# Attention of a macaron block: one division for two groups of heads, places from a running count

## What is computed

```python
q1, q2, k1, k2 = projections of x and of x with the token before   # 16 heads, 4 numbers each
L_q, L_k = exterior(q1, q2), exterior(k1, k2)                      # 6 numbers a head, normed
attn = jnp.einsum('bqhc,bkhc->bhqk', L_q, L_k @ J6.T) * 6 ** -0.5
attn = softmax(where(causal, attn, -inf))                          # over the keys
out = einsum('bhqk,bkhd->bqhd', attn, (x @ W_v + b_v) by heads)    # 16 numbers a head
x = x + out @ W_o + b_o
```

## Time and profile before

| | us |
|---|---|
| median of 3 runs | 1180.17 (1180.03 to 1180.23) |
| the profiled execution, its time | 1177.99 |
| the profiled execution, its span | 1176.3 |
| PE busy in the span | 1036.9 (88%) |
| ACT busy | 884.8 (75%) |
| DVE busy | 774.8 (66%) |
| POOL busy | 435.5 (37%) |
| mean granted clock of TensorE | 0.982 of full speed |

### The profile page before, as it was taken

How to read it: one execution, slowest core, us unless ns; L and a number is a source line. 1 busy time by engine, 2 the same in 40 slices (tenths; PEclk the granted TensorE clock), 3 DMA queues, 4 the chain that set the end, 5 groups by cost and what they waited for, 6 DMA issues and landing times.

```text
span 1176.3 us, 23514 instructions
## 1 busy us (share of the span) xinstructions
PE 1036.9 (88%) x7487; PEld 557.7 (47%) x7487; DVE 774.8 (66%) x1565; ACT 884.8 (75%) x1314; POOL 435.5 (37%) x531
## 2 busy tenths in 40 slices
PE   4998999898886888998889898988889998999996
PEld 3457999755553211222122122222123568898854
DVE  6897777768996314443244557476579778777866
ACT  4336777646888999999999999989998336677720
POOL 1004666377720323321111122430121435577755
PEclk9999999989998899999999999999999999999998
DMA  8902555446766101010201022020200854566655
GB/s 289 289 27 60 166 172 167 144 121 197 214 193 215 52 20 53 19 50 10 64 10 46 23 69 76 22 80 8 58 1 1 272 185 149 158 185 186 178 170 152
DMA packets 125716, 133.78 MB, mean 114 GB/s; under 512 B 13224, under 2 KB 111888, under 8 KB 125616
## 3 DMA queue, kind: packets, MB, share of 16 engines
q1 hardware_dynamic: 109056, 90.95, 24.5%
q0 software_dynamic: 14448, 39.47, 12.2%
q10 hardware_dynamic: 2112, 2.10, 0.5%
HBM read 80.43 MB, written 52.04 MB: 113 GB/s over the span
## 4 chain that ended last, share of the span: by engine, by line
PE 25%; ACT 23%; issue 19%; DVE 9%; POOL 2%; DVEq 1%; DMA 1%; ACTq 0%; POOLq 0%
ACT wide L2021 21%; PE banks L2388 6%; PE banks L2313 4%; PE banks L1905 3%; PE banks L2400 3%; PE banks L1880 2%; POOL f_region L1341 2%; PE banks L2322 2%; PE banks L1919 1%; PE banks L2376 1%; DVE x_res L1595 1%; DVE wide L1622 1%; DVEq L2596 1%; PE banks L1433 1%; DVE attn_lines_parts L202 1%
## 5 line engine op out<-in xcount | busy, mean ns | idle before, releaser
L2021 ACT ACTIVATE wide<-banks 128x1536 f32<-128x1536 f32 (+1 forms) x448 | 505.5, 1282 | 14.6 <-PE banks L1880 14.4
L1905 PE MATMUL banks<-wide,attn_attend_v_now 128*32 128x512 f32 (+3 forms) x2560 | 298.6, 542 | 0.1
L2037 POOL TENSOR_SCALAR_AFFINE_SELECT wide<-wide 128x512 f32<-128x512 f32 (+2 forms) x176 | 89.5, 523 | 444.3 <-ACT wide L2021 443.9
L1880 PE MATMUL banks<-attn_attend_q_now,attn_attend_k_now 32*128 32x512 f16 (+3 forms) x1280 | 158.8, 357 | 68.1 <-ACT wide L2021 64.3
L1880 PEld LDWEIGHTS banks<-attn_attend_q_now,attn_attend_k_now 32*128 32x128 f16 x1280 | 43.2, 91 | 321.2 <-ACT wide L2021 297.6
L651 POOL DMA_INDIRECT f_region<-xn_rows,f_token_of x79 | 79.1, 1001 | 126.0 <-DVE f_token_of L882 83.7
L2388 PE MATMUL banks<-f_xnt 128*128 128x128 f32 x752 | 101.7, 278 | 9.8 <-DVE f_more L2614 7.2
L2074 DVE RECIPROCAL below<-below 128x512 f32<-128x512 f32 x32 | 107.3, 3353 | 1.1
L2388 PEld LDWEIGHTS banks<-f_xnt 128*128 128x128 f32 x752 | 91.3, 191 | 15.3 <-ACT f_xnt L2466 8.8
L2069 DVE COPY sums<-banks 128x512 f32<-128x512 f32 x32 | 22.1, 691 | 109.9 <-PE banks L1905 109.1
L2496 POOL DMA_INDIRECT last_rows_in<-xn_rows,f_spare x72 | 69.7, 968 | 64.3 <-DVE f_stage L2557 23.7
(11 more groups left out here) (365 smaller groups left out, 1774.1 us busy)
## 6 DMA issues: line engine op xcount, KB each, us to landing
y_half<-f_xnt SPq DMA_DIRECT2D x94, 128.0 KB
y_slots<-wide SPq DMA_DIRECT2D x79, 128.0 KB, 1.7
attn_v<-f_more SPq DMA_DIRECT2D x32, 256.0 KB, 3.7
attn_attend_v_now<-attn_v SPq DMA_DIRECT2D x32, 256.0 KB, 3.1
x_res<-L_attn_x SPq DMA_DIRECT2D x8, 512.0 KB, 7.6
xn_rows<-f_w_all SPq DMA_DIRECT2D x8, 512.0 KB, 4.5
attn_q<-attn_lines_q_out SPq DMA_DIRECT2D x8, 512.0 KB, 3.4
attn_k<-attn_lines_k_out SPq DMA_DIRECT2D x8, 512.0 KB, 4.0
```

What stands on the lines that cost most here:

```text
L1880: last = pe.matmul(score[i % SLOTS][:, j, c0:QW], k_now[rows, kt * P:(kt + 1) * P], q_now[rows, qc * QW + c0:(qc + 1) * QW], start=True, s ...
L1905: last = pe.matmul(out_bank[qc][rows, c0:QW], v_now[:, kt, rows], probs[:, place_of[HG * u + h], c0:QW], start=(kt == 0), stop=(u == last_ ...
L2021: act.activation(probs[:, at:at + n, c0:QW], score[i % SLOTS][:, 0:n, c0:QW], ACT.Exp, scale=SCALE).then_inc(sem.exp_done, 1)
L2037: pool.affine_select(out=part, in_=part, compare_op=ALU.is_ge, fill=0.0, base=0, pattern=[[0, end - begin], [1, P]], channel_multiplier=-1 ...
```

## The change

It has these parts:

- `plan_groups` makes a plan for each group. The number of strips may be any (strips_of loses its `multiple`), and a strip's place in `probs` and its score slot come from a running count over all groups (`base`). Steps that were fixed numbers are mapped by `at(g, i)` from a grid that holds the old chunk starts (0, 6, 17, 34, 56).
- One division for the two groups of a pair. Side 0's chunk is only copied into `heads`. Side 1's chunk picks numerators and sums out of the two by `holds`, shuffles, divides and multiplies once.
- VectorE's program in the attention is written by steps (`step`) rather than by chunks, but for group 7 (`last_group`). `route_first` is divided into `route_chunk` and `route_step`.
- The table BY_VECTOR can name units whose exponential VectorE makes by a polynomial (`exponential`, `score_for_vector`, `weigh_by_vector`, `scale_values`). All eight entries of it are empty.
- `load_shared` comes behind group 6 on SP's queue (before: behind group 5).
- mask_turn, stat_turn, shuffle_turn and load_turn are one semaphore, `turn`; `divided` is gone. A tensor `sixth` of 512 columns is added.

```diff
+GRID = (0, 6, 17, 34, 56)
+BY_VECTOR = (
+    (),
...
-def strips_of(first_columns, wide, multiple):
+def strips_of(first_columns, wide):
...
-    taken = min((m for m in best[count] if m % multiple == 0), key=lambda m: best[count][m][0])
+    taken = min(best[count], key=lambda m: best[count][m][0])
...
+def plan_groups(units, last_of, diagonal):
+
+    plans, base, done, masked, before = [], 0, 0, 0, 0
+    for g in range(BATCH * GROUPS):
+        by_vector = {u: (score_steps, step) for u, score_steps, step in BY_VECTOR[g]}
+        items = [(u, h) for u in range(len(units)) if u not in by_vector for h in range(HG)]
+        strips = strips_of([units[u][2] for u, _ in items], STRIP_WIDE)
+        strip_of = [i for i, (_, n, _) in enumerate(strips) for _ in range(n)]
+        column = [j for _, n, _ in strips for j in range(n)]
+        places = {item: (base + i) % STRIP_RING * STRIP_WIDE + j for item, i, j in zip(items, strip_of, column)}
...
+    def at(g, i):
+
+        qc = max(qc for qc in range(QC) if GRID[qc] <= i)
+        first = plans[g].first
+        return first[qc] + (i - GRID[qc]) * (first[qc + 1] - first[qc]) // (GRID[qc + 1] - GRID[qc])
...
-            if g == GATE + 1:
+            if g == GATE + 2:
                 load_shared(sp)
...
+        def scores_read():
+
+            if scored[0] > 0:
+                pe.wait_ge(sem.vector_step, 3 * scored[0] - 1)
...
         def chunk(g, side, two, qc):
 
-            dve.wait_ge(sem.pv_done, U * g + last_of[qc] + 1)
-            if later(g) or qc > 0:
-                dve.wait_ge(sem.divided, QC * g + qc)
-            if side and qc > 0:
+            dve.wait_ge(sem.pv_done, plans[g].counts[last_of[qc]])
+            part, own, other = heads[:, qc, :], holds[:, 0:1], holds[:, 1:2]
+            if side == 0:
+                dve.tensor_copy(part, out_bank[qc]).then_inc(sem.sums_kept, 1)
+                dve.wait_ge(sem.sums_kept, QC * g + qc + 1)
+                return
+            if two > 0 or qc > 0:
                 dve.wait_ge(sem.heads_ready, QC * two + qc)
-            elif not side and qc == 0 and later(g):
-                dve.wait_ge(sem.heads_ready, QC * two)
             dve.tensor_copy(sums[:], out_bank[qc]).then_inc(sem.sums_kept, 1)
             dve.wait_ge(sem.sums_kept, QC * g + qc + 1)
-            dve.sem_inc(sem.shuffle_turn, 1)
-            dve.stream_shuffle(below[:], sums[:], [(1 - side) * DH] * HR).then_inc(sem.chain_step, 1)
-            dve.wait_ge(sem.chain_step, 2 * (QC * g + qc) + 1)
-            dve.reciprocal(below[:], below[:]).then_inc(sem.chain_step, 1)
-            dve.wait_ge(sem.chain_step, 2 * (QC * g + qc) + 2)
-            into = sums[:] if side else heads[:, qc, :]
-            dve.scalar_tensor_tensor(into, sums[:], holds[:, side:side + 1], below[:], ALU.mult, ALU.mult).then_inc(sem.divided, 1)
-            if side:
-                dve.wait_ge(sem.divided, QC * g + qc + 1)
-                dve.tensor_tensor(heads[:, qc, :], heads[:, qc, :], sums[:], ALU.add).then_inc(sem.heads_ready, 1)
+            chain(dve.tensor_scalar(below[:], sums[:], own, None, ALU.mult))
+            chain(dve.scalar_tensor_tensor(below[:], part, other, below[:], ALU.mult, ALU.add))
+            chain(dve.tensor_scalar(part, part, own, None, ALU.mult))
+            chain(dve.scalar_tensor_tensor(part, sums[:], other, part, ALU.mult, ALU.add))
+            dve.sem_inc(sem.turn, 1)
+            chain(dve.stream_shuffle(sums[:], below[:], [DH] * DH + [0] * DH))
+            chain(dve.reciprocal(sums[:], sums[:]))
+            dve.tensor_tensor(part, part, sums[:], ALU.mult).then_inc(sem.heads_ready, 1)
...
+        def step(g, side, two, i):
+
+            if later(g) and length(g - 1) + i == plans[g - 1].ends[QC - 1]:
+                chunk(g - 1, 1 - side, two - 1 if side == 0 else two, QC - 1)
+            for qc in range(QC - 1):
+                if plans[g].ends[qc] == i:
+                    chunk(g, side, two, qc)
+                    route_chunk(g, qc)
+            for qc, half in project_at[g].get(i, ()):
+                of = two - 1 if qc == QC - 1 else two
+                add_half(of, qc, half)
+                if half:
+                    add_up(of, qc)
...
+            route_step(g, i)
+            for u, _, n in plans[g].scored_at.get(i, ()):
+                exponential(g, i, u, n)
```

More of the change, by code:

```diff
@@ new lines, in weighed, with projections_of @@
+    def weighed(g, i):
+        first, n, _ = plans[g].strips[i]
+        return plans[g].counts[list(plans[g].places)[first + n - 1][0]]
+    two_of_0, four_of_1 = ((0, 0), (0, 1)), ((1, 0), (1, 1), (2, 0), (2, 1))
+    GATE = GROUPS
+    def projections_of(g):
+        steps = PROJECT_7 if g % 2 == 0 else PROJECT_7 + (PROJECT_6_LATE if g == GATE + 1 else PROJECT_6)
+        parts = ((QC - 1, 0), (QC - 1, 1)) if g % 2 == 0 else two_of_0 + four_of_1
+        placed = {}
+        for i, part in zip(steps, parts):
+            if g > 0:
+                placed.setdefault(at(g, i), []).append(part)
+        return placed
@@ L1747, in attend @@
+    project_at = [projections_of(g) for g in range(ALL)]
     proj_bank = lambda qc, half: banks[:, 7 if qc in (0, QC - 1) else 6, :]
@@ L1774, in place @@
+    for g, plan in enumerate(plans):
+        begins = [plan.steps[last_of[qc - 1] + 1 if qc else 0] for qc in range(QC)]
+        for i in plan.scored_at:
+            assert i < begins[0] or plan.ends[0] < i < begins[2] or plan.ends[1] < i < begins[3] or plan.ends[2] < i
     def place(g):
@@ L1876, in scores @@
-            for j in range(n):
-                qc, kt, _ = units[(first + j) // HG]
-                h = (first + j) % HG
+            if plan.base + i >= SLOTS:
+                pe.wait_ge(sem.exp_done, plan.base + i - SLOTS + 1)
+            items = list(plan.places)[plan.strips[i][0]:plan.strips[i][0] + n]
+            for j, (u, h) in enumerate(items):
+                qc, kt, _ = units[u]
                 rows = slice(h * HR, (h + 1) * HR)
-                last = pe.matmul(score[i % SLOTS][:, j, c0:QW], k_now[rows, kt * P:(kt + 1) * P],
+                last = pe.matmul(score[(plan.base + i) % SLOTS][:, j, c0:QW], k_now[rows, kt * P:(kt + 1) * P],
@@ new lines, in weigh_by_vector @@
+        def weigh_by_vector(g, u):
+            qc, kt, _ = units[u]
+            n = vector_units.index((g, u))
+            pe.wait_ge(sem.vector_step, 3 * HG * (n + 1))
+            pe.wait_ge(sem.v_scaled, n + 1)
+            held = lambda h: (HG * n + h) % (2 * HG)
+            scaled = v_scaled[n % HG]
+            for h in range(HG):
+                rows = slice(h * HR, (h + 1) * HR)
+                pe.matmul(out_bank[qc][rows, :], v_now[:, kt, rows], core.one[:].to_broadcast([P, QW]), start=False, stop=False)
+            for h in range(HG):
+                rows = slice(h * HR, (h + 1) * HR)
+                pe.matmul(out_bank[qc][rows, :], scaled[:, 0, rows], squares[held(h)], start=False, stop=False)
+            for h in range(HG):
+                rows = slice(h * HR, (h + 1) * HR)
+                last = pe.matmul(out_bank[qc][rows, :], scaled[:, 1, rows], sixths[held(h)], start=False, stop=False)
+            last.then_inc(sem.pv_done, 1)
@@ L2187, in group @@
[L2187 to L2192 removed]
+                route_chunk(g, qc)
+                if qc == 1:
+                    add(two, 0)
+                    dve.wait_ge(sem.stats_done, 3 * QC - 3)
+                    routing.statistics(dve, HT, BT)
+                elif qc == 2:
+                    add_among_marks(two)
@@ L2195, in vector, with group @@
+        def group(g, side, two):
+            if g == ALL - 1:
+                return last_group(g, side, two)
+            for i in range(length(g)):
+                step(g, side, two, i)
         dve.tensor_reduce(holds[:, 0:1], core.ident[:].rearrange("p (j r) -> p j r", r=HR)[:, :, 0:DH], mybir.AxisListType.XY, ALU.add)
```

331 lines of the change are left out of this document (208 added, 123 removed).

## The result

| | before | after |
|---|---|---|
| median, us | 1180.10 of 4 runs (1178.20 to 1180.23) | 1190.05 of 4 runs (1189.91 to 1192.89) |
| profiled execution: time, span | 1177.99, 1176.3 | 1190.17, 1187.4 |
| DVE busy in the span | 774.8 | 730.6 |
| PE busy, ACT busy | 1036.9, 884.8 | 1041.4, 886.1 |

After over before is 1.0094 (95%: 1.0076 to 1.0112), formed from the single runs; the medians differ by 10.0 us, which is 1.0084. The forecast was 6.4 us slower, so the sign was right and the size was not; 1190.05 lies 0.55 above the upper end of the range.

The account below looks back on a forecast made before the run. ScalarE's exponential was taken to bound the attention, and after 905 us VectorE's last division, then TensorE's last projection and a TensorE-bound stage. 0.9 + 2.4 + 3.1 = 6.4 us on 1180.2 gave 1186.6; range 1182.5 to 1189.5.

Parts of the forecast that it names:

- Parts costed at nothing: Strip plan, empty BY_VECTOR, VectorE's order by steps, later shared loads and merged turn semaphores: claimed to leave the time alone.
- The chain: VectorE's side 1 work from chunk copy to finished heads: claimed 1.8 us longer (1.7 to 2.3), 8.3 where GpSimd rests.
- (a): Start of group 5: TensorE waits for VectorE's copy of a tile behind chunk (5,0); 0.9 us lost.
- (b): Logits in group 5: GpSimd's bias additions hold VectorE's scalings, TensorE's transposes wait 3.5 us; 2.4 lost.
- the first rival: GpSimd does not hold the chain, so (b) is nothing; 1184.2, or 1183.8 with the lesser chain; chance 0.27.
- scores that came early: Within (b) at group 5's logits: an estimated 0.7 us of TensorE's wait that ScalarE does not see.
- (c): End of group 7: late projection costs ScalarE 1.3 us; with the 1.8 longer chain the last projection starts 3.1 later.
- The third rival: Slower by more: tensor_scalar at 0.78 makes the chain 2.3 longer, 8.4 us in all, 1188.6; chance 0.08.
- The second: No measurable change: the last stage takes up the shift at 913; 1181.1, to 1182.2 with half of (c); chance 0.13.
- The fourth: Faster: the 82 us side 0 gives back shorten a ScalarE wait, likely at group starts; 1177.3; chance 0.07.

Follow-up runs that it names:

- Experiment 1: The changed kernel with the old two divisions in all pairs of groups, the rest of the change kept; 0.9973 of the kernel before.
- experiment 8: The changed kernel with side 0's masked halves and side 1's sums formed straight from PSUM, still one division; 0.9992 of the kernel before.
- experiment 10: The changed kernel without side 1's reciprocal, heads multiplied with the sums instead of divided; 1.0008 of the kernel before.
- experiment 9: The changed kernel with an unused shuffle, reciprocal and scaling added behind each side 0 copy; 1.0105 of the kernel before.
- experiment 6: The changed kernel with GpSimd's four bias additions moved from the second chunk of group 5 into that of group 6; 1.0003 of the kernel before.
- run 12: The changed kernel once more, no edit, for its profile; one time, 1189.05 against 1179.64 for the kernel before (1.008).
- experiment 4: The changed kernel with the old two divisions in the third pair alone (groups 4 and 5); 1.0017 of the kernel before.
- experiment 11: experiment 8 with the last chunk's reciprocal and multiplication in two halves, each released to the last projection by itself; 1.0006, 1181.49 against 1179.64 for the kernel before.
- experiment 3: The changed kernel with the old two divisions in the last pair alone (groups 6 and 7); 1.0049 of the kernel before.
- experiment 7: The changed kernel with six unread TensorE matmuls put ahead of the last projection; 1.0062 of the kernel before.
- run 5: The changed kernel again, no edit, as reference for the runs beside it; 1.0066 of the kernel before.

## Why the prediction was right in sign and short in size

**Parts costed at nothing: right.** Experiment 1 has them all and shows no step.

**The chain: right.** A tensor_scalar of 128x512 took 0.49 (forecast 0.53 with its gap, here 0.52), the whole chain 8.3 us. It is the length of this chain on side 1, not the number of divisions, that counts: experiments 8 and 10 shorten it and all three terms vanish, experiment 9 puts side 0's work back and nothing changes.

**(a) 0.9: measured 0.80 to 0.83.** Place and cause as named; the cover was 0.1 thicker than read.

**(b) 2.4: place and cause right, size too small.** GpSimd does hold the chain (experiment 6), so the first rival is out. Two steps of the term were off and nearly cancelled, which is luck: TensorE waited 2.94, not 3.5, and at strip 46 ScalarE was spared some 0.5, not 1.1. That gives the 2.38 seen. What was missing stands behind the wait: 1.0 at strip 47 and 0.64 at strip 52. The first is the clock: the sum took every matmul after a wait at the duration of the kernel before. The second is cover that the term took off as saved and that was only lent: of its 1.1 us, the 0.37 in which TensorE had stood idle were saved, the 0.7 for "scores that came early" came back five strips later. At full clock (b) would have been about 2.6 (TensorE's transposes 3.00 us late, less 0.37), and the clock made it 4.0 here, 5.0 in run 12. The step that failed is "2.4 are lost": the term was 4.0.

**(c) 1.3 in group 7: measured 1.6. 1.8 to the last projection: measured 1.81.** The prediction then wrote "All of what follows hangs on it ... so I take nothing back: 3.1". It took nothing back, rightly (experiments 4 and 6 carry 1.8 on through the matmuls behind it), but it also added nothing: TensorE idles 2.94 us there where it idled 1.14, and its clock fell to half for the stretch behind, 1.8 us more. This is the larger part of the miss.

Together: 1.6 in (b), 1.8 behind (c), 0.4 in (c) with the small steps, less 0.1 in (a) and 0.2 at strip 16 of group 6, make 3.5; 6.4 + 3.5 = 9.9, against 10.0 between the medians. That the two agree so well is chance: this one profile is 11.1 us longer than the other, and 1.3 of it stand in the two entries at the top of that table. They are not the change's: in run 12 the first strip is 0.06 late, the strips come 0.81 earlier from strip 7 of group 0 on and 1.33 later from strip 8 of group 4 on, and experiment 11, which keeps none of the changed kernel's losses in groups 5 and 7, has 0.9 at the same strips 21 and 22 of group 0.

That the clock moves could be read from the kernel before. Its windows at the start of the attention, where TensorE comes out of a stretch in which it was busy for half the time:

```profile
380.00:385.00 5.00, 2.58 (x22) 1.25 (x22) 2.07 (x8) 4.83 (x8) 1.82 (x4) 0.50 0.10 34
385.00:390.00 5.00, 5.00 (x33) 1.43 (x33) 0.00 (x0) 3.74 (x4) 1.39 (x3) 0.60 0.01 3
390.00:395.00 5.00, 3.57 (x44) 0.92 (x41) 3.38 (x4) 5.00 (x5) 0.00 (x0) 1.00 0.31 107
```

In the second, TensorE is busy throughout with 33 matmul records at a clock of 0.60. I had not cut the stage into such windows.

The third rival (longer chain) came nearest by its number, 1188.6, but not by its mechanism: the chain was as short as in the forecast. The second left out (b) from its sum without a reason, and its 1182.2 is less than half of (c) would give (1180.2 + 0.9 + 1.55 = 1182.7); the runs show that no part of the 1.8 at the last projection is taken up within the 60 us behind it. The fourth is out: experiment 9 shows no gain from side 0's time. Range and chances rested on bounds for VectorE's operations alone. Nothing in them let TensorE's own speed change, though the earlier trace rows show a mean clock of 0.99 and 0.97.

**What stays open.** When the clock falls behind a wait. Behind the logits it fell in all six profiles that have that wait (the changed kernel three times, experiments 3, 7 and 9). Behind the last wait of 2.9 to 3.3 us it fell in full in three (changed, run 5, experiment 9), in part in one (run 12), and not in two (experiments 4 and 6). These two are also those without the wait at the logits, 150 us earlier. That may be chance; no run here separates it, and so the 1.8 us are measured where they occur, but not forecastable. It also fell in groups 0, 3 and 4 of seven profiles with no added wait of TensorE ahead of it, so that the wait causes the fall is likely at the logits (six of six with it, none in the eight profiles without it) and not shown at the last projection. A run that takes the wait at the logits away by other means than the additions, and one that fills exactly 2.9 us ahead of the last projection, are missing.

The Trainium skill (TensorE: Matmul & The Clock Gate, Part 1) says that the throttled clock is the default, that the engine's recent activity releases it, and that the count of slow matmuls differs from run to run of one kernel. The trace agrees that the count differs: 3.75 or 1.97 us for the same projection behind the same wait. That activity releases the clock fits 0.50, 0.60 and 1.00 in the three windows above. No run shows which level is the default, and experiments 4 and 6 stood idle for 2.95 us and kept 1.00.

## What to carry to other kernels

Count the length of each chain that somebody waits for, not the work that is saved: a division shared by two producers leaves the queue of the one nobody waits for and makes the last one's chain longer, and here VectorE's 44 us less went with 10 us of loss. Where a change adds a wait to TensorE, add behind it the price of its lower clock, read from a stretch of the trace that has one (here 0 to 1.8 us for a wait of 2.9), as an end of the range. Where a wait is covered in part, ask whether the cover is idle time, which is saved, or work done ahead, which comes back at the next dense place. Beside elementwise work of GpSimd, prefer operations of VectorE that read PSUM, and keep scalings of SBUF tensors out of its time.

## What the runs showed of the hardware

- GpSimd's additions (four of 128x1024, 9.37 us alone) held VectorE's tensor_scalar as well as its operations on two SBUF tensors: 1.95 and 2.50 us instead of 0.49, and 2.73 instead of 0.75. The two engines took turns: the three held operations ended at 752.58, 755.35 and 757.88, each 0.28 to 0.54 us behind the end of one of GpSimd's additions (752.30, 754.81, 757.60), and GpSimd's four took 10.01. Not held: stream_shuffle (0.77), reciprocal (3.35), and scalar_tensor_tensor with one operand in PSUM (0.75 and 0.74). The Trainium skill (GPSIMD Engine Reference, 1. Specifications) names two classes of VectorE operations for the contention, those with two SBUF inputs and those in a 2-port mode. The trace agrees for two inputs; that tensor_scalar was held fits the second, though no row here shows an operation's mode.
- The same eight matmuls of 128x256 took 1.97 us or 3.75 behind the same wait of 2.95 us, at granted clocks of 1.00 and 0.50.
- A reciprocal of 128x256 took 1.74, one of 128x512 3.35: halving it costs 0.13 us in all.
